# Layers 0 and 1 of an attention kernel: values of a context from one 80-row product, spread by a 0/1 tile, taken on ScalarE

## The chip, the cores and the metric

The kernel is one program on one core of a Trainium2 chip. The metric is device time in microseconds, the median of several executions. The core's engines each run their own instruction stream and meet through semaphores: TensorE (PE; its weight loads appear as PEld), VectorE (DVE), ScalarE (ACT), GpSimd (POOL) and SyncE (SP), which issues most DMAs.

## What is computed

The reference is four layers, each a cross attention and a feed-forward part with residuals, on x of 4 x 1024 x 256. Everything the change touches is in the attention of layers 0 and 1, on a context of 77 rows per batch:

```python
x = x + L0_xattn(layernorm(x), ctx, ctx, Wq, bq, Wk, bk, Wv, bv, Wo, bo)   # 16 heads of 16
x = x + L0_ffn(layernorm(x), ...)                                          # routed splines, gamma, beta
x = x + L1_xattn(layernorm(x), ctx, ctx, ...)                              # keys and values shared by the heads
# inside both attentions:
k = ctx @ Wk + bk ; v = ctx @ Wv + bv      # once per batch: 77 rows
attn = softmax(q @ k.T / 4) ; out = attn @ v
```

Layer 0 has 256 value columns (16 per head); layer 1 has 16, used by all heads. Layer 1's mask is causal. Layers 1 to 3 go on with two expert layers and a last attention; the change leaves them alone.

## The kernel before

`attention_layers` does layers 0 and 1. The 4096 rows of x are cut into 8 halves (NH = 8) of 512 tokens, two halves to a batch and so to a context. The program on every engine is the same double loop: `for h in range(-1, NH + 3)` and in it 16 slots (`PERIOD`), and each engine's code says what it issues in which slot. In round h, slots 0 to 7 hold the eight attention units of layer 0 on half h, slots 8 to 15 the eight units of layer 1 on half h-2 (rounds 0 and 1 have none there). A unit is 128 tokens by 8 heads: scores on TensorE (L176), maximum and shift on VectorE (L1007, L1008), exponential on ScalarE (L719), sums on VectorE (L1013, L1014), normalising on GpSimd (L631), five transposes on TensorE (L871), a copy to `PT` on ScalarE (L730), the value products on TensorE (L188) and a copy to `OT` on ScalarE (L726). The last four steps come two slots after the scores. Between the units lie the queries, norms and outputs: in slots 10 to 15 the output product of layer 0 (`project_out`, L840), the transposes of the next half's normalised rows (L826), the copy to `XT` (`take_xt`, L708), the query product (`project_q`, L833), its copy (`take_q`, L713), and the norm of the half's new rows (`ln_stats` L1018, `root` L698 on ScalarE, `ln_rstd` L1028 to L1033 on VectorE, `apply` L703 on ScalarE). Each round's norm "a" goes: statistics in slot 12, root in slot 13, `ln_rstd` in slot 13 behind `shift` and `sums`, `apply` in slot 14. GpSimd waits in slot 14 for `scale_by_gamma` (L1102), which VectorE issues in slot 13 behind `ln_rstd`.

Every instruction of an engine stands in line: a wait for one holds all behind it.

Keys and values of a context are made four times: for context 0 in round -1 (slots 0 to 5), and for contexts 1, 2, 3 in slots 10 to 15 of rounds 0, 2 and 4 (`context_of`). The value products of the units need the values of a context row repeated for 8 heads: 8 heads x 80 rows are 640 rows, in 5 blocks of 128 (`BLK`), so that each head's rows can be masked to that head's columns. Before the change this repetition is made at the input: `replicate` (L736, ScalarE) copies the transposed context 8 times to `crep`; `keys` on TensorE waits for it, makes the keys (L881, L883), the five 16-column value blocks of layer 1 (L887) and the last 256-column block of layer 0 (L889); `values` (L895) makes the other four blocks in two portions, two blocks in slot 12 and two in slot 14 (context 0: all in slot 4). Each block is two products, since the 256 inputs are two chunks of 128. ScalarE takes the keys (`take_keys`, L745, L746). VectorE takes the values with their bias to `vtmp` and `v1tmp` (`take_keys` and `take_values` there, L1120, L1126). GpSimd masks them to `Kbd` and `Vbd` (L649, L658, L668, L670) in the next round. All of these use the two banks called `wide` (SC). In the trace an f32 product is two MATMUL records, so L887 has 20 records a context, L889 4, L895 16.

The set-up block ahead of it loads the weights, and GpSimd makes masks there with `affine_select` (L476).

## Time and profile before

| | us |
|---|---|
| median of 3 executions | 2973.98 (2966.57 to 2975.74) |
| profiled execution, its time | 2977.86 |
| its span in the trace | 2976.1 |
| PE busy / DVE busy / ACT busy / POOL busy | 2417.7 / 1962.4 / 1508.6 / 809.2 |

Busy shares of the whole span say little here: the stages follow one another with barriers between, and the change lies in the first, from 28 to 776 us. Within it the starts of L1007 on VectorE, one per slot with a unit, are a clock by which slots can be compared between rounds: a round with a context (0, 2, 4) with one without.

### The profile page before, as it was taken

Reading aid. Unit: us, or ns where it says so; the run is one execution under the profiler, and the core shown is the slowest. Engines: PE = TensorE matmul, PEld = TensorE weight load, DVE = VectorE, ACT = ScalarE, POOL = GpSimd, SP = SyncE. Lnnn points to the kernel's source line nnn. Section 1 sums busy time; section 2 is a strip of 40 time slices with the busy share of each in tenths; the row PEclk is TensorE's granted clock in tenths of the full one; section 3 lists DMA queues with packets and bytes.
Section 4 is the critical chain, followed back from the end, with each engine's and each line's share of the span. In section 5 each row is a group of like instructions: output and inputs, shape, how many; then the busy total and the mean of one; then the engine's idle time right before and its main releaser. Section 6 shows DMA issues by size and latency. Waiting matters only on the chain. (4 is left out here: it accounts for less than half of the span.)

```text
span 2976.1 us, 43560 instructions
## 1 busy us (share of the span) xinstructions
PE 2417.7 (81%) x16502; PEld 1975.3 (66%) x16502; DVE 1962.4 (66%) x4449; ACT 1508.6 (51%) x2566; POOL 809.2 (27%) x707
## 2 busy tenths in 40 slices
PE   4778888877589999999849999999999276767665
PEld 3545554544477887888739999999999255555544
DVE  4688878875556666666526566666664468686867
ACT  2456667653445665565425444444543255545443
POOL 2233434432222433444440000000000572626030
PEclk9788888886699999999969999999999698988887
DMA  7500000000100111100014334333441511211000
GB/s 234 208 1 16 15 1 15 8 8 15 38 1 1 44 35 38 36 20 15 20 66 134 118 124 140 127 117 118 139 134 57 166 47 35 63 33 57 1 15 15
DMA packets 152616, 184.22 MB, mean 62 GB/s; under 512 B 21560, under 2 KB 118101, under 8 KB 152408
## 3 DMA queue, kind: packets, MB, share of 16 engines
q1 hardware_dynamic: 139400, 154.16, 15.8%
q0 software_dynamic: 12288, 27.15, 2.9%
q8 instruction: 132, 2.16, 0.3%
q14 instruction: 76, 0.62, 0.1%
q10 hardware_dynamic: 720, 0.12, 0.0%
HBM read 116.38 MB, written 71.43 MB: 63 GB/s over the span
## 5 line engine op out<-in xcount | busy, mean ns | idle before, releaser
L2355 POOL DMA_INDIRECT picked<-expert_out,so x128 | 126.8, 990 | 866.3 <-DMA so<-slots 765.1
L157 PE MATMUL SC<-Xhi,Whi 128*128 128x320 f32 x1024 | 319.9, 312 | 7.1 <-DVE Wlo L2148 5.3
L157 PE MATMUL SC<-Xlo,Whi 128*128 128x320 f32 x1024 | 316.9, 310 | 0.0
L157 PE MATMUL SC<-Xhi,Wlo 128*128 128x320 f32 x1024 | 316.9, 309 | 0.0
L631 POOL TENSOR_TENSOR PR<-PR,rs 128x616 f32<-128x616 f32 x128 | 157.8, 1233 | 410.0 <-DVE rs L1014 410.0
L1384 POOL TENSOR_TENSOR ff_Hlo<-ff_HF,ff_Hhi 128x512 fp32r<-128x512 f32 x112 | 148.0, 1322 | 419.4 <-ACT ff_Hhi L1517 419.3
L2125 ACT ACTIVATE Hhi<-HF 128x320 fp32r<-128x320 f32 x256 | 120.7, 471 | 154.7 <-DVE HF L2178 154.7
L157 PEld LDWEIGHTS SC<-Xhi,Whi 128*128 128x128 f32 x1024 | 193.0, 188 | 7.8 <-DVE Wlo L2148 5.7
L2167 DVE TENSOR_TENSOR Hlo<-HF,Hhi 128x320 fp32r<-128x320 f32 x256 | 125.5, 490 | 104.3 <-ACT Hhi L2125 104.3
L2148 DVE TENSOR_TENSOR Wlo<-Wraw,Whi 128x1024 fp32r<-128x1024 f32 x96 | 114.6, 1223 | 119.2 <-ACT Whi L2113 119.2
L157 PEld LDWEIGHTS SC<-Xlo,Whi 128*128 128x128 f32 x1024 | 193.1, 189 | 0.0
L157 PEld LDWEIGHTS SC<-Xhi,Wlo 128*128 128x128 f32 x1024 | 192.7, 188 | 0.0
L1784 DVE TENSOR_TENSOR ff_HF<-raw,SC 128x512 f32<-128x512 f32 x112 | 76.7, 685 | 168.3 <-ACT raw L1511 115.2
L157 PE MATMUL GP<-Whi,Hhi 128*128 128x256 f32 x640 | 181.8, 284 | 2.1 <-issue 2.1
L157 PE MATMUL GP<-Wlo,Hhi 128*128 128x256 f32 x640 | 181.8, 284 | 0.0
L157 PE MATMUL GP<-Whi,Hlo 128*128 128x256 f32 x640 | 181.8, 284 | 0.0
L176 PE MATMUL SC<-Kbd,QT 64*128 64x308 f32 x512 | 121.5, 556 | 66.3 <-DVE PR L1008 62.7
L2136 ACT ACTIVATE SG<-SC 128x320 f32<-128x320 f32 x256 | 111.5, 436 | 107.5 <-PE SC L157 107.5
L2178 DVE TENSOR_TENSOR HF<-SG,SC 128x320 f32<-128x320 f32 x256 | 124.2, 485 | 53.0 <-ACT SG L2136 52.8
L2113 ACT ACTIVATE Whi<-Wraw 128x1024 fp32r<-128x1024 f32 x96 | 97.3, 1048 | 115.6 <-PE GP L157 115.1
L871 PE MATMUL GP<-ident,PR 128*128 128x128 f32 x640 | 113.2, 317 | 44.1 <-ACT OT L726 27.6
L730 ACT ACTIVATE PT<-GP 128x640 f32<-128x640 f32 x128 | 89.5, 699 | 115.7 <-PE GP L871 115.3
(477 smaller groups left out, 6979.4 us busy)
## 6 DMA issues: line engine op xcount, KB each, us to landing
expert_in<-zeros SPq DMA_DIRECT2D x4, 5120.0 KB, 32.7
rowsin<-expert_in SPq DMA_DIRECT2D x32, 640.0 KB, 6.0
expert_out<-rowsout SPq DMA_DIRECT2D x32, 640.0 KB, 4.0
Wraw<-L_wg SPq DMA_DIRECT2D x32, 512.0 KB, 7.0
Wraw<-L_wu SPq DMA_DIRECT2D x32, 512.0 KB, 7.2
Wraw<-L_wd SPq DMA_DIRECT2D x32, 512.0 KB, 7.9
X<-x SPq DMA_DIRECT2D x8, 512.0 KB, 4.3
x_after_l_attention<-X SPq DMA_DIRECT2D x8, 512.0 KB, 2.8
```

Source lines behind the costliest of these rows:

```text
L157: last = nc.tensor.matmul(out, lhs[l], rhs[r], start=start and n == 0, stop=stop and n == 2)
L176: last = nc.tensor.matmul(o[j], q[r], K[r, 4 * j:4 * j + 4, 0:CTX], start=mask is None, stop=True)
L631: nc.gpsimd.tensor_tensor(pr, pr, bc_last(rs[n % NPA][:, :], CTX), mult).then_inc(pnorm, 1)
L871: last = nc.tensor.transpose(ptrans[:, k * P:(k + 1) * P], pr[:, k * P:(k + 1) * P], ident[:, :])
L1384: nc.gpsimd.tensor_tensor(lo[:, :], HF[q % 2][:, :], hi[:, :].bitcast(f32), ALU.subtract).then_inc(h_low, 1)
L2113: nc.scalar.activation(Wsp[j % 2][0][:, n, :], Wraw[j % 2][:, n, :], ACT.Copy).then_inc(w_high, 1)
L2125: nc.scalar.activation(Hsp[q // NU % 2][0][:, h, n * CC:(n + 1) * CC], HF[q % 2][:, :], ACT.Copy).then_inc(h_high, 1)
L2136: nc.scalar.activation(SG[u % 2][:, :], SC[u % 2][:, 0:CC], ACT.Silu).then_inc(s_ready, 1)
L2148: nc.vector.tensor_tensor(Wsp[j % 2][1][:, n, :], Wraw[j % 2][:, n, :], Wsp[j % 2][0][:, n, :].bitcast(f32), ALU.subtract)\
L2167: nc.vector.tensor_tensor(lo_, HF[q % 2][:, :], hi_.bitcast(f32), ALU.subtract).then_inc(h_made, 1)
L2178: nc.vector.tensor_tensor(HF[u % 2][:, :], SG[u % 2][:, :], SC[u % 2][:, 512:512 + CC], ALU.mult).then_inc(h_mult, 1)
L2355: nc.gpsimd.indirect_dma_start(picked[g][:, t, k, :], None, oute[:, :], bass.IndirectOffsetOnAxis(ap=so[g][:, t, k:k + 1], axis=0)).then_i ...
```

## The change

- `crep` and its copy are gone. A third product of `keys` multiplies the context itself (80 rows as output rows) with the value weights of both layers side by side (`wv`, 272 columns).
- VectorE adds the biases on the way to a tile `vctx` of 80 x 272 (`add_value_bias`, slot 12; context 0: slot 2), one instruction in place of three.
- A 0/1 tile `spread` of 80 x 5 x 128, made in the set-up block, repeats the rows: `last_values` (slot 12; context 0: slot 3) makes the last block of layer 0 and the five of layer 1, `values` (slot 14; context 0: slot 4) the other four blocks, all in one go and only when ScalarE has taken what `last_values` made.
- ScalarE takes the values: `take_last_values` in slot 13 and `take_values` in slot 15; its `take_keys` goes from slot 11 to 12, behind `take_xt` (context 0: slots 3, 5 and 2).
- `ln_rstd` of norm "a" on VectorE goes from slot 13, behind `shift` and `sums`, to the head of slot 14, ahead of `shift`; `scale_by_gamma` stays in slot 13.

```diff
                     def keys(b):
-                        pe.wait_ge(crep_ready, b + 1)
+                        if b:
+                            pe.wait_ge(ctx_in, 16 * b)
...
-                        for j in range(BLK):
-                            for k in range(KC):
-                                nc.tensor.matmul(wide[:, V1AT + j * DH:V1AT + (j + 1) * DH], rep(j, k), wv1[:, k, :], start=k == 0, stop=k == KC - 1)
                         for k in range(KC):
-                            last = nc.tensor.matmul(wide[:, TOK:TOK + D], rep(BLK - 1, k), wv0[:, k, :], start=k == 0, stop=k == KC - 1)
+                            last = nc.tensor.matmul(wide[0:CTXP, TOK:TOK + D + DH], ctxT[:, k, :], wv[:, k, :], start=k == 0, stop=k == KC - 1)
                         last.then_inc(k_psum, 1)
-                    def values(j0, j1):
-                        for j in range(j0, j1):
-                            for k in range(KC):
-                                last = nc.tensor.matmul(wide[:, j * D:(j + 1) * D], rep(j, k), wv0[:, k, :], start=k == 0, stop=k == KC - 1)
-                        return last
+                    def last_values(b):
+                        pe.wait_ge(vctx_ready, b + 1)
+                        nc.tensor.matmul(wide[:, TOK:TOK + D], spread[:, BLK - 1, :], vctx[:, 0:D], start=True, stop=True)
+                        for j in range(BLK):
+                            last = nc.tensor.matmul(wide[:, V1AT + j * DH:V1AT + (j + 1) * DH], spread[:, j, :], vctx[:, D:], start=True, stop=True)
+                        last.then_inc(v4_psum, 1)
+
+                    def values(b):
+                        pe.wait_ge(kcol_ready, b + 1)
+                        pe.wait_ge(v4_taken, b + 1)
+                        for j in range(BLK - 1):
+                            last = nc.tensor.matmul(wide[:, j * D:(j + 1) * D], spread[:, j, :], vctx[:, 0:D], start=True, stop=True)
+                        last.then_inc(v_psum, 1)
...
+                    def take_last_values(b):
+                        act.wait_ge(v4_psum, b + 1)
...
+                        nc.scalar.activation(vtmp[:, BLK - 1, :], wide[:, TOK:TOK + D], ACT.Copy)
+                        nc.scalar.activation(v1tmp[b % 2][:, :, :], wide[:, V1AT:V1AT + BLK * DH].rearrange("p (j d) -> p j d", d=DH), ACT.Copy)\
+                            .then_inc(v4_taken, 1)
+                    def take_values(b):
+                        act.wait_ge(v_psum, b + 1)
+                        nc.scalar.activation(vtmp[:, 0:BLK - 1, :], wide[:, :].rearrange("p (j d) -> p j d", d=D), ACT.Copy).then_inc(v_taken, 1)
...
+                for h in range(HH):
+                    keep_where(spread[:, :, :], [[P, BLK], [1, P]], -CTXP * h, -1, ALU.not_equal, 1.0)
...
+                            if s == 14 and 0 <= h < NH:
+                                ln_rstd(h, LN["a"], var_a, sd_a, rstd_a)
                             if now is not None:
                                 shift(now)
```

On TensorE in round 4 (context 3), slots 11 to 12, what stood in a row before:

```order
L881 MATMUL SC1<-ctxT,wk0 128x80 x4
L883 MATMUL SC1<-ctxT,wk1r 128x80 x2
L887 MATMUL SC1<-wv1,crep 128x16 x10
L889 MATMUL SC1<-wv0,crep 128x256 x2
L871 MATMUL GP0<-ident,PR2 128x128 x5
```

and what stands there now:

```order
L892 MATMUL SC1<-ctxT,wk0 128x80 x4
L894 MATMUL SC1<-ctxT,wk1r 128x80 x2
L897 MATMUL SC1<-wv,ctxT 80x272 x2
L884 MATMUL GP0<-ident,PR2 128x128 x5
```

Twelve products became two; six new ones (L902, L904) stand one slot later, behind the transposes of `XP`, where four of L895 stood.

On ScalarE in the same round, slots 11 to 14, before (PR0 is the unit of slot 12, PR1 of slot 13; `root` is L698):

```order
L745 ACTIVATE kcol0<-SC1,bk0c 128x80 x2
L746 ACTIVATE kcol1_1<-SC1,bk1c 128x80
L703 ACTIVATE XN_1<-XN_1,nm_g,rstd_g 128x256 x4
L730 ACTIVATE PT<-GP0 128x640
L719 ACTIVATE PR0<-PR0 128x8x77
L726 ACTIVATE OT_1<-GP0 128x128
L708 ACTIVATE XT<-GP1 128x1024
L730 ACTIVATE PT<-GP0 128x640
L698 ACT_TABLE_LOAD
L698 ACTIVATE sd_a<-mv_a,eps 128x4
```

and now, to the same root:

```order
L706 ACTIVATE XN_1<-XN_1,nm_g,rstd_g 128x256 x4
L733 ACTIVATE PT<-GP0 128x640
L722 ACTIVATE PR0<-PR0 128x8x77
L729 ACTIVATE OT_1<-GP0 128x128
L711 ACTIVATE XT<-GP1 128x1024
L742 ACTIVATE kcol0<-SC1,bk0c 128x80 x2
L743 ACTIVATE kcol1_1<-SC1,bk1c 128x80
L733 ACTIVATE PT<-GP0 128x640
L701 ACT_TABLE_LOAD
L701 ACTIVATE sd_a<-mv_a,eps 128x4
```

The taking of the keys went from ahead of `XN_1`, PT and the exponential to behind `XT`; `crep` (one slot earlier, L736) is gone.

On VectorE in the same round, slots 13 and 14, now (before, L1028 to L1033 stood ahead of `XN_1` times gamma, and L1007 behind it):

```order
L1116 TENSOR_TENSOR XN_1<-XN_1,gammar 128x1024
L1042 RECIPROCAL rstd_a<-sd_a 128x4
L1043 TENSOR_TENSOR nw_a<-rstd_a 128x4
L1044 SCALAR_TENSOR_TENSOR nw_a<-mv_a,nw_a 128x4
L1045 TENSOR_SCALAR nw_a<-nw_a 128x4
L1046 TENSOR_TENSOR rstd_a<-rstd_a,nw_a 128x4
L1047 SCALAR_TENSOR_TENSOR nm_a<-mv_a,rstd_a 128x4
L1021 TENSOR_REDUCE mx<-SC0 128x8
```

Only the product with gamma passed the norm; the norm's place to the next `shift` is the same.

## Rows read from the trace of the kernel before

**Rows 1.** Busy by stretch: start:end, length, busy of each engine, clock, DMA
```profile
28.00:776.00 748.00, 587.49 (x4384) 377.66 (x4384) 567.54 (x1329) 434.19 (x735) 264.86 (x212) 0.84 0.13 47
```

**Rows 2.** Waits of 28 to 776: waiter, released by, total us, times, longest
```profile
ACT kcol L745 <- PE SC L889: 23.0, 4, 7.5
...
DVE rstd_a L1028 <- ACT sd_a L698: 20.5, 8, 6.4
```

**Rows 3.** Groups by line and shape: busy, mean ns, idle before them
```profile
L708 ACT ACTIVATE XT<-GP 128x1024 f32<-128x1024 f32 x24 | 24.6, 1025 | 24.9 <-PE GP L826 24.8
...
L736 ACT ACTIVATE crep<-ctxT 128x1280 f32<-128x1280 f32 x4 | 5.0, 1258 | 0.0
```

**Rows 4.** Timeline of context 0: start, us, engine, what [idle before]
```profile
26.68 1.41 DVE L1018 BATCH_NORM_STATS2 stats_p<-X 128x6 f32<-128x256 f32 x4 [0.90 <-PEq L79]
...
30.04 2.00 PE L881 MATMUL SC<-ctxT,wk 128*128 128x80 f32 x8 [5.42 <-ACT crep L736]
30.14 2.07 ACT L703 ACTIVATE XP<-X,nm_p,rstd_p 128x256 f32<-128x256 f32 x4 [0.15 <-DVE nm_p L1033]
...
32.68 4.37 PE L887 MATMUL SC<-wv,crep 128*128 128x16 f32 x20
...
36.88 2.05 PE L889 MATMUL SC<-wv,crep 128*128 128x256 f32 x4
...
41.31 3.70 PE L833 MATMUL GP<-XT,wq 128*128 128x512 f32 x8 [1.11 <-ACT XT L708]
...
48.40 0.79 PE L176 MATMUL SC<-Kbd,QT 64*128 64x308 f32 x4
```

**Rows 5.** Timeline of round 4, slots 12 to 14 (context 3)
```profile
388.65 0.80 DVE L1007 TENSOR_REDUCE mx<-SC 128x8 f32<-128x616 f32 x1 [0.32 <-PE SC L176]
...
390.51 2.34 PE L887 MATMUL SC<-wv,crep 128*128 128x16 f32 x20
...
393.85 0.55 ACT L745 ACTIVATE kcol<-SC,bk0c 128x80 f32<-128x80 f32 x2 [4.33 <-PE SC L889]
...
396.12 0.77 DVE L1007 TENSOR_REDUCE mx<-SC 128x8 f32<-128x616 f32 x1
...
407.50 0.79 DVE L1007 TENSOR_REDUCE mx<-SC 128x8 f32<-128x616 f32 x1
...
410.47 1.99 PE L895 MATMUL SC<-wv,crep 128*128 128x256 f32 x8
...
410.79 2.06 ACT L703 ACTIVATE XN<-X,nm_a,rstd_a 128x256 f32<-128x256 f32 x4
```

**Rows 6.** Timeline of round 5, slots 12 to 14 (no context)
```profile
474.84 0.79 DVE L1007 TENSOR_REDUCE mx<-SC 128x8 f32<-128x616 f32 x1
...
479.00 0.77 DVE L1007 TENSOR_REDUCE mx<-SC 128x8 f32<-128x616 f32 x1
...
483.32 0.18 DVE L1028 RECIPROCAL rstd_a<-sd_a 128x4 f32<-128x4 f32 x1 [1.78 <-ACT sd_a L698]
...
485.54 0.79 DVE L1007 TENSOR_REDUCE mx<-SC 128x8 f32<-128x616 f32 x1
...
485.98 1.27 ACT L713 ACTIVATE QT<-GP,bq0c 128x512 f32<-128x512 f32 x2 [0.56 <-PE GP L833]
```

**Rows 7.** Timeline of round 0, slots 12 to 14 (context 1)
```profile
88.48 1.01 PE L881 MATMUL SC<-ctxT,wk 128*128 128x80 f32 x8
...
99.20 1.89 PE L895 MATMUL SC<-wv,crep 128*128 128x256 f32 x8
...
104.91 1.28 ACT L719 ACT_TABLE_LOAD   x1
```

**Rows 8.** Timeline elsewhere: a slow query product, and the set-up block's masks
```profile
5.25 0.26 POOL L476 TENSOR_SCALAR_AFFINE_SELECT causal<-causal 128x77 bf16<-128x77 bf16 x1
...
6.21 0.10 POOL L493 MEMSET edge<- 128x1 f32 x1
...
665.57 6.42 PE L833 MATMUL GP<-XT,wq 128*128 128x512 f32 x8 [1.11 <-ACT XT L708]
```

More of the change, by code:

```diff
@@ L395, in attention_layers @@
         causal = sb("causal", [P, CTX], bf16)
-        crep = sb("crep", [P, KC, HH, CTXP])
+        spread = sb("spread", [CTXP, BLK, P])
+        vctx = sb("vctx", [CTXP, D + DH])
         vtmp = sb("vtmp", [P, BLK, D])
@@ L478, in _ @@
                 for t, v in ((ident[:, :], 0.0), (identb[:, :], 0.0), (headof[:, :], 1.0), (blockhead[:, :, :], 1.0),
-                             (onesf[:, :], 1.0), (onesb[:, :], 1.0), (before[:, :], 1.0), (causal[:, :], 0.0)):
+                             (onesf[:, :], 1.0), (onesb[:, :], 1.0), (before[:, :], 1.0), (causal[:, :], 0.0),
+                             (spread[:, :, :], 0.0)):
                     link(nc.gpsimd.memset(t, v))
@@ L802, in _ @@
                                 take_one_hot(c1)
-                            if s == (0 if c == 0 else 10) and c is not None:
-                                replicate(c)
                             if p < NH and s == query_slot(p, "apply"):
                                 apply(p, rstd_p, XP, X[p % NXA], LN["p"], xn_p)
-                            if s == (1 if c == 0 else 11) and c is not None:
-                                take_keys(c)
                             if s == 11 and 0 <= c1 < NH:
@@ L818, in _ @@
                                 take_xt(h, xt_a_psum, xt_a)
+                            if s == (2 if c == 0 else 12) and c is not None:
+                                take_keys(c)
+                            if s == (3 if c == 0 else 13) and c is not None:
+                                take_last_values(c)
+                            if s == (5 if c == 0 else 15) and c is not None:
+                                take_values(c)
                 @block.tensor
@@ L872, in unit_transposes @@
                         last.then_inc(pt_psum, 1)
[L874 to L875 removed]
                     def keys(b):
[L878 removed]
+                        if b:
+                            pe.wait_ge(ctx_in, 16 * b)
                         for c in range(KC):
@@ L984, in _ @@
                                 project_q(wq0, p, xt_p, q0_psum)
-                            if s == (4 if c == 0 else 12) and c is not None:
-                                pe.wait_ge(kcol_ready, c + 1)
-                                values(0, BLK // 2)
+                            if s == (3 if c == 0 else 12) and c is not None:
+                                last_values(c)
                             if s == (4 if c == 0 else 14) and c is not None:
-                                pe.wait_ge(v4_taken, 2 * (c + 1))
-                                values(BLK // 2, BLK - 1).then_inc(v_psum, 1)
+                                values(c)
                             if s == 15 and 0 <= h < NH:
@@ L1165, in _ @@
                                 ln_stats(XN[c1 % G], LN["g"], var_g)
-                            if s == (5 if c == 0 else 15) and c is not None:
-                                take_values(c, 0, BLK - 1, wide[:, :], v_psum, v_taken)
                             if s == 10 and 0 <= c1 < NH:
@@ L1174, in _ @@
                                 ln_stats(X[h % NXA], LN["a"], var_a)
-                            if s == 13 and 0 <= h < NH:
-                                ln_rstd(h, LN["a"], var_a, sd_a, rstd_a)
                             if s == 13 and 0 <= c1 < NH:
```

55 lines of the change are left out of this document (22 added, 33 removed).

## The prediction, written before the changed kernel was run

> **What bounds the kernel now.** I read the busy times by stretch first. In the stage of layers 0 and 1, 748 us of the span, PE is busy 587 us, DVE 568, ACT 434 [rows 1]: no engine is full, so the stage is a ring of waits, and what counts is where each wait ends last. The starts of L1007 show the ring's pace. In round 5, without a context, slot 12 takes 4.2 us (474.84 to 479.00) and slot 13 takes 6.5 (to 485.54) [rows 6]; in round 4, with one, the same slots take 7.5 and 11.4 [rows 5]. Round 2 reads like round 4. So a context costs about 8.2 us in each of these two rounds, whichever engine does its work. The waits name the places: ACT waits 23.0 us in four times for the last product of `keys`, DVE 20.5 us in eight times for the root of norm "a" [rows 2], and PE 5.42 us once for `crep` [rows 4]. The stage's end is a barrier, so what is gained up to there is gained to the end.
>
> **Removed work.** Per context PE loses 20 records of L887, 4 of L889 and 16 of L895, and gains 4 (272 columns), 2 (256), 10 (16) and 8 (256). At the rates of round 4 a 16-column record takes 0.117 us (2.34 for 20) and a 256-column record 0.24 (1.99 for 8, with its end) [rows 5]. In `keys` 24 records (2.3 + 0.9 = 3.2 us) become 4 of about 0.25, 1.0 us: 2.2 us less ahead of everything in slot 12. `last_values` is 2 x 0.24 + 10 x 0.117 = 1.6 us, `values` 8 x 0.24 = 1.9. A contraction over 80 rows in place of 128 is not in the trace; its record is bounded by the 16-column one (0.117) and the 256-column one at the slow rate (0.51, from 2.05 for 4 [rows 4]); I take 0.24, since the moving columns are the same. ACT loses `crep` (1.26 us) and gains takes of 256, 80 and 1024 columns. 1024 columns cost 1.02 us [rows 3]; the small two lie between 0 and 1.02 together, and I take 0.7 by columns and a fixed part. DVE exchanges three instructions for one.
>
> **Context 0, term 1.** PE starts 30.04, after 5.42 us of idling for `crep` [rows 4]. Without `crep` it starts when the block does, about 26.7, as DVE's L1018 shows [rows 4]. Keys take 2.0 + 1.1 us, the new product 2.0 at the slow rate seen here: done at 31.8. The transposes of XP wait for ACT's L703, which doesn't move (30.14 to 32.21 [rows 4]); they run 32.3 to 33.8, XT is taken by 34.9, the query product runs 3.7 us to 38.7, `last_values` to 40.3, its takes to 41.1, `values` to 43.1. The first scores start at 43.1 in place of 48.40 [rows 4]: 5.3 us. ACT's `take_values` (1.0 us) and its table load lie beside the scores and `shift`. What may eat into it is PE's clock: the first 8 us of this stretch ran at half speed, L887 taking 4.37 us for 20 records [rows 4] where round 4 takes 2.34 [rows 5]. If the query product, `last_values` and `values` ran so, it would cost 6.42 - 3.70 = 2.7 [rows 4, 8], 1.5 and 1.5: 5.7 us. Between 0 and 5.7 I take 1.0, since L833 ran at 3.70 after a wait of 1.11 [rows 4]. **Term 1: -4.3 us** (0 to -5.3).
>
> **Context 1, term 2.** Round 0 has no units in slots 8 to 15, so this is a bare chain. `keys` ends 2.1 us sooner, at 91.0 (it starts 88.48 [rows 7], which doesn't move: `project_out` ends there). Transposes of XP to 91.9, `last_values` to 93.4, XT to 92.9, keys taken by 93.9, query product 93.4 to 97.1, its take to 98.5. Only then comes ACT's `take_last_values`, to 99.2, and `values` on PE waits for it, for its banks: it starts at 99.2, where the second portion of L895 starts now [rows 7]. The 2.1 us are lost in that wait. Behind it ACT has `apply` and XT about 1.0 us sooner, and then `take_values` with 1.02 us ahead of the table load at 104.91 [rows 7]. **Term 2: 0 us** (-1 to +1.5).
>
> **Contexts 2 and 3, term 3.** Followed in round 4. `keys` is done at 391.7 in place of 393.8. ACT no longer waits 4.33 us for it ahead of XN, PT and the exponential [rows 5]: XN runs 389.6 to 391.6, PT to 393.0, exponential to 393.7, OT to 394.1. PE: values of the unit to 393.8, XP to 394.8, `last_values` to 396.3. ACT: XT to 395.9, keys to 396.8. Slot 13: PE transposes to 397.1, ACT PT to 397.8, root with its table load to 399.4, load and exponential to 401.4; PE's query product 398.5 to 402.2; ACT takes it by 403.5, then the small value takes, 0.7, to 404.2, where `take_last_values` now stands ahead of PT. Slot 14: PT to 404.9, exponential to 405.6, PE's unit products to 405.6, `values` to 407.3 (its wait is long over), OT, and `apply` of norm "a" starts at 406.0 in place of 410.79 [rows 5]: 4.8 us. In slot 15 ACT gets `take_values`, 1.02 us [rows 3], ahead of slot 0's PT: 3.85 us remain. The chain from there to the next round runs on ACT, through XT, PT and root "c", so DVE's larger gain (it loses L1120) isn't added. Bounds: 0, if the new takes hold ACT as long as the wait did; 8.2, if a context came to cost nothing. **Term 3: 2 x -3.85 = -7.7 us** (0 to -16.4).
>
> **The norm a slot later, term 4.** In round 5 DVE waits 1.78 us at L1028 [rows 6] with the product with gamma (1.2 us) behind it. Now the product fills the wait, and `shift` of slot 14 starts 1.1 us sooner. But ACT in slot 14 starts with L713 at 485.98, after 0.56 us of idling for PE's L833 [rows 6], and then takes PT and the exponential; L833 depends on XT, not on this norm. What DVE gains ends in its wait for the exponential or for root "c". In round 4 the wait of 6.4 us [rows 2] is part of term 3. **Term 4: 0 us** (0 to 8 x -1.1 = -8.8, the lower end if it all passed on).
>
> **At nothing.** GpSimd makes `spread` with one memset and 8 selects of 640 columns; 77 columns cost 0.26 us [rows 8], so at most 8 x 2.2 = 17.6 us if it goes by columns alone. GpSimd has finished its masks at 6.3 [rows 8], and the set-up block, which waits for the weights, holds PE's work until 24.6 (30.04 less 5.42): 18.3 us of cover. Without it, it would be 2 (8 x 0.26) to 17.6 us. The split load of `wv` moves the same bytes. SP's `context` wait comes sooner, with nothing behind it that was late.
>
> **Sum.** -4.3 + 0 - 7.7 + 0 = **-12.0 us** against the profiled execution's own 2977.86, so 2965.9; that execution lies 3.9 us above the median of the runs shown, so the forecast against the median is 2962.0.
>
> **Rivals.** (A) *The norm's 1.1 us passes on in all eight rounds*: -8.8 more, 2953. For it: DVE's 20.5 us of waiting [rows 2]. Against: ACT's slot 14 starts on PE. 13%. (B) *ACT becomes the bound in rounds 2 and 4*: the new takes stand ahead of PT and XT there, and gain is left of about 1 us each: -4.3 - 2 = -6.3, 2968. For it: `apply`, XT, PT, exponential already stand in a row; against: the 4.33 us wait goes for certain. 22%. (C) *Not what it says at the start*: the block is held by something else than `crep`, term 1 is 0: -7.7, 2966. 5%. (D) *Slower*: the engine that loses 20 us of work falls to half clock at the contexts. Then the query product, `last_values` and `values` cost 5.7 us more at each of the four, all on the chain: 22.8 against the undiscounted 13.0, +9.8, 2984. It decides from three of four contexts on. For it: L833 at 6.42 us late in the stage, behind waits [rows 8]; against: rounds without a context have less PE work in these slots and L833 there runs 3.7. 5%.
>
> The Trainium skill, page "TensorE: Matmul & The Clock Gate", section "Loop structure matters more than you think", says that a stretch in which TensorE idles brings its clock back down, which speaks against a change that takes work from it. By that rule, the trace agrees at 665.57 us, where L833 took 6.42 us behind a wait, and not at 41.31, where it took 3.70 behind one as long. By the page case (D) would be the outcome and the sum +9.8; by the rows of context 0 it isn't.
>
> **How the numbers follow.** The forecast has 55%, with its own range of 2957 to 2967 (term 1 and term 3 within a third). The range for 8 in 10 goes from 2951 (case A with its undiscounted start, and the spread of the medians) to 2971 (case B with term 1 at its small end), leaving out (D). 0.3% is 8.9 us, about what a measurement of this kernel can tell from no change: faster by more holds A and nine tenths of the forecast and a little of C, 66%; within 0.3% holds B, C and the forecast's rest, 28%; slower 6%.
>
> **What the profile after would show.** Term 1: first scores (L176) near 43 to 45, PE's first product before 28. Term 2: exponential's table load in round 0 behind the first scores by about 4 us, as now. Term 3: slots 12 and 13 of rounds 2 and 4 at together 13 to 16 us in place of 19; the waits for L889 gone. Term 4: rstd_a waits under 5 us in all, while rounds 3 and 5 keep their length of 78 to 79 us. If plain rounds get shorter, (A); if rounds 2 and 4 keep 19 us, (B); if L833 reads above 5 us at the contexts, (D).

## The result, and the profile after

| | before | after |
|---|---|---|
| median | 2972.61 (2965.56 to 2975.74) | 2947.76 (2940.64 to 2950.61) |
| ratio | | 0.992 [0.9903, 0.9937] |
| profiled execution, its time / span | 2977.86 / 2976.1 | 2950.61 / 2948.8 |

All times are us; each side has five executions. The change is faster by 0.8%, 24.9 us between the medians; the forecast was 2962.0 and the range ended at 2951, so the result lies outside it, on the fast side. Two more comparisons with copies of both kernels, each on one chip (below), give 18.7 and 19.5 us, 0.62% and 0.69%.

The stage of layers 0 and 1 is the part of the program that the change edits. Its busy times after, by stretch (start:end, length, busy of PE, PEld, DVE, ACT, POOL with counts, granted clock, DMA share, GB/s):

```profile
28.00:764.00 736.00, 573.49 (x4317) 362.81 (x4316) 562.98 (x1322) 434.95 (x743) 270.20 (x212) 0.84 0.14 49
```

Beside [rows 1] PE has 14 us less work and DVE 5 less, ACT has as much as before, at the same mean clock. The waits of the same stretch (waiter, releaser: total, times, longest):

```profile
ACT PT L733 <- PE GP L884: 114.9, 69, 5.0
...
DVE rstd_c L1042 <- ACT sd_c L701: 20.4, 8, 4.7
...
DVE rstd_a L1042 <- ACT sd_a L701: 6.5, 6, 1.8
```

ACT's wait for the last product of `keys`, 23.0 us in [rows 2], doesn't appear any more; DVE's wait for the root of norm "a" went from 20.5 us to 6.5. Context 0 after (start, us, engine, line, idle before with its releaser):

```profile
27.06 1.97 PE L892 MATMUL SC<-ctxT,wk 128*128 128x80 f32 x8 [2.06 <-PEq L79]
...
29.68 2.02 PE L897 MATMUL SC<-wv,ctxT 128*80 128x272 f32 x4
...
32.65 1.97 PE L839 MATMUL GP<-ident,XP 128*128 128x128 f32 x8 [0.95 <-ACT XP L706]
...
35.73 6.03 PE L846 MATMUL GP<-XT,wq 128*128 128x512 f32 x8 [1.11 <-ACT XT L711]
...
41.59 0.60 PE L902 MATMUL SC<-vctx,spread 80*128 80x256 f32 x2
...
42.03 1.18 PE L904 MATMUL SC<-vctx,spread 80*128 80x16 f32 x10
...
43.91 1.97 PE L911 MATMUL SC<-vctx,spread 80*128 80x256 f32 x8 [0.69 <-ACT v1tmp L752]
...
45.80 0.79 PE L176 MATMUL SC<-Kbd,QT 64*128 64x308 f32 x4
```

Beside [rows 4]: PE starts 3.0 us earlier, as it should without `crep`, but the first scores come only 2.6 us earlier, 45.80 for 48.40: the query product, 3.70 us before, takes 6.03. Round 4, slots 12 to 14, after:

```profile
379.62 0.80 DVE L1021 TENSOR_REDUCE mx<-SC 128x8 f32<-128x616 f32 x1 [0.32 <-PE SC L176]
...
381.48 1.08 PE L897 MATMUL SC<-wv,ctxT 128*80 128x272 f32 x4
...
384.68 0.77 DVE L1021 TENSOR_REDUCE mx<-SC 128x8 f32<-128x616 f32 x1
...
386.52 0.54 ACT L742 ACTIVATE kcol<-SC,bk0c 128x80 f32<-128x80 f32 x2
...
388.98 3.70 PE L846 MATMUL GP<-XT,wq 128*128 128x512 f32 x8
...
391.15 0.80 DVE L1021 TENSOR_REDUCE mx<-SC 128x8 f32<-128x616 f32 x1
...
393.87 0.38 ACT L751 ACTIVATE vtmp<-SC 128x256 f32<-128x256 f32 x1
394.13 0.25 ACT L752 ACTIVATE v1tmp<-SC 128x80 f32<-128x80 f32 x1
...
395.91 2.06 ACT L706 ACTIVATE XN<-X,nm_a,rstd_a 128x256 f32<-128x256 f32 x4
```

Slots 12 and 13 take 5.1 and 6.5 us, 11.5 together, where they took 7.5 and 11.4 in [rows 5]; `take_keys` (L742) waits for nothing; `apply` of norm "a" starts 16.3 us after slot 12 and not 22.1.

**Where the time went**, from the starts of the slots' first instructions (L1007 before, L1021 after; a round is taken at its slot 1, rounds 8 and 9 at slot 8; the last mark before the span's end is ScalarE's first instruction of the next stage). Each number is how much earlier than before that point comes:

| point | before | after | earlier by |
|---|---|---|---|
| first `shift` | 49.6 | 46.6 | 3.0 |
| round 1 | | | 3.4 |
| round 2 / round 3 | | | 2.3 / 7.2 |
| round 4 / round 5 | | | 8.7 / 14.1 |
| rounds 6, 7, 8, 9 | | | 13.9, 16.4, 12.9, 15.1 |
| next stage begins | 780.3 | 764.8 | 15.5 |
| end of the span | 2976.1 | 2948.8 | 27.3 |

Rounds 2 and 4, which hold contexts 2 and 3, gain 4.9 and 5.4 us; the start 3.0; context 1 0.4; the rest moves to and fro by up to 3.5 and adds up to 1.8. That is 15.5 us in the edited stage. The other 11.8 of the profiled pair lie behind it, in stages that no edit touches (start:end as above, the next stage in both kernels and then the last):

```profile
780.30:1535.70 755.40, 669.91 (x3748) 567.22 (x3748) 470.14 (x1543) 410.53 (x621) 290.76 (x240) 0.94 0.08 25
...
2314.80:2976.10 661.30, 430.73 (x3042) 309.56 (x3042) 461.11 (x795) 301.33 (x533) 238.34 (x221) 0.86 0.16 48
```

```profile
764.80:1517.60 752.80, 668.10 (x3748) 566.44 (x3748) 469.65 (x1543) 410.47 (x621) 290.46 (x240) 0.94 0.08 26
...
2296.10:2948.80 652.70, 430.73 (x3042) 310.89 (x3042) 461.23 (x795) 300.47 (x533) 237.79 (x221) 0.85 0.16 48
```

The instruction counts are the same, PE's busy time in the last stage is the same to 0.01 us, and yet it is 8.6 us longer in the execution of before. Of the seventeen profiled executions of this study, only that one shows a last stage over 654.

### The profile page after: what moved, and what is told of

It is laid out like the page before. It is cut to its first block and busy times, and to the rows that moved or that the text cites. A ratio compares the mean times of both kernels' runs of the same rounds, so it can differ in the third digit from the quotient of the medians.

```text
span 2948.8 us, 43447 instructions
## 1 busy us (share of the span) xinstructions
PE 2401.7 (81%) x16438; PEld 1960.9 (66%) x16438; DVE 1957.3 (66%) x4441; ACT 1508.3 (51%) x2574; POOL 820.3 (28%) x716
## 3 DMA queue, kind: packets, MB, share of 16 engines
q1 hardware_dynamic: 139304, 154.11, 15.9%
## 5 line engine op out<-in xcount | busy, mean ns | idle before, releaser
L2360 POOL DMA_INDIRECT picked<-expert_out,so x128 | 126.4, 987 | 864.7 <-DMA so<-slots 764.5
```

The source lines that it names most:

```text
L2360: nc.gpsimd.indirect_dma_start(picked[g][:, t, k, :], None, oute[:, :], bass.IndirectOffsetOnAxis(ap=so[g][:, t, k:k + 1], axis=0)).then_i ...
```

## The experiments

Fifteen kernels ran, in four groups; those of a group ran on the same chip and share the executions of before. Each ratio is against before in that group. "Stage" is the end of layers 0 and 1 in the profiled execution: 780.3 before, 764.8 after.

### Group 1: taking the change apart

**e1_norm_only**, the kernel before with norm "a" a slot later:

```diff
+                            if s == 14 and 0 <= h < NH:
+                                ln_rstd(h, LN["a"], var_a, sd_a, rstd_a)
                             if now is not None:
                                 shift(now)
...
-                            if s == 13 and 0 <= h < NH:
-                                ln_rstd(h, LN["a"], var_a, sd_a, rstd_a)
```

> The kernel before, with only the norm of each round (ln_rstd of norm a) moved to the head of slot 14. Theory 1 (what VectorE gains ends in ScalarE's chain): rounds 3 and 5 keep 78 to 79 us, the whole 0 to 2 us under the kernel before. Theory 2 (the 1.1 us passes on in each of eight rounds, rival A): 9 us under it, the rounds near 77.5. If the later stages, which no edit touches, are shorter by 9 to 12 us here too, they are so whatever is edited.

Measured: 2963.44, ratio 0.9981 [0.997, 0.9992]; stage ends at 773.9. From slot 12 to slot 1 of the next round, the plain round 3 takes 22.9 us in place of 23.4, the context rounds 31.1 in place of 31.2. It is a small gain in plain rounds and hardly any where a context is; the ratio lies between the two recorded theories (0 to 2 us, and 9). The stage ends 6.4 us sooner, more than these rounds add up to, although its first scores come 1.7 us later (the query product takes 5.34 us here, see group 4). But e10 below, the kernel before with nothing changed behind the set-up block, also ends its stage 4.4 us sooner, so the length of this one stage can't be read as the norm's worth.

**e2_no_norm**, the changed kernel with the norm back in slot 13 (the same four lines, reversed):

> The changed kernel with the norm back in slot 13. Theory 1: within 2 us of the changed kernel, so 23 to 25 us under the kernel before; in rounds 2 and 4 slot 13 stays long, as the root comes late, but the chain runs on ScalarE. Theory 2: 9 us above the changed kernel.

Measured: 2949.1, 0.9938 [0.9917, 0.9958]; stage ends at 764.1, against 764.8 with the norm moved. The median is 19.0 us under that of before, where 23 to 25 were expected. Everything else of the change holds its gain without it: the moved norm is worth nothing that can be seen in the median or the stage's end. It isn't a clean nothing: this execution's start was 2.3 us shorter by TensorE's clock (first `shift` at 44.3 for 46.6, group 4), and from there on the stage takes 719.8 us against 718.2.

**e3_dve_takes**, the changed kernel with the same two takes as copies on VectorE, in the same slots:

```diff
-                        nc.scalar.activation(vtmp[:, 0:BLK - 1, :], wide[:, :].rearrange("p (j d) -> p j d", d=D), ACT.Copy).then_inc(v_taken, 1)
+                        nc.vector.tensor_copy(vtmp[:, 0:BLK - 1, :], wide[:, :].rearrange("p (j d) -> p j d", d=D)).then_inc(v_taken, 1)
```

> The changed kernel with the values taken by VectorE copies, in the same slots (13 and 15; 3 and 5 at the start). Theory 1 (ScalarE's chain is the bound in rounds 2 and 4, and the takes there cost 1.7 us each): 2 to 4 us faster than the changed kernel, if VectorE's slots stay beside it. Rival (VectorE is the bound): 2 to 4 us slower.

Measured: 2948.23, 0.9929 [0.9914, 0.9945]; the stage ends at 759.4, 5.4 us before that of the changed kernel. Slot 12 to slot 1 of the context rounds is 24.6 us, against 26.4. Of the 5.4 us, 0.9 stand at the start, where TensorE's clock rose sooner; from the first `shift` on the stage takes 713.7 us against 718.2, and in the two later pairs with and without these takes 711.0 against 721.4 (e11, e9) and 708.0 against 711.6 (e15, e14). In the median it can't be told from its neighbours. So in the traces one of the moves in the change costs: the takes on ScalarE stand ahead of `PT`, and in slot 15 ahead of the next one. VectorE has room there (round 4 of this kernel):

```profile
394.44 1.23 DVE L1130 COPY vtmp<-SC 128x1024 f32<-128x1024 f32 x1 [0.67 <-PE SC L893]
```

It waits 0.67 us for the product and copies in 1.23. ScalarE's take of the same tile lasts 1.02, but on the chain.

**e4_with_crep**, the changed kernel in which ScalarE still makes `crep`, that nobody reads, and the first products still wait for it:

```diff
-                        if b:
-                            pe.wait_ge(ctx_in, 16 * b)
+                        pe.wait_ge(crep_ready, b + 1)
```

> The changed kernel with the copy of the context for 8 heads (nobody reads it) made again on ScalarE, and the first products waiting for it as before. Term 1 (the start): the first scores come 3.0 to 3.4 us later than in the changed kernel, and the rest is unchanged, since at rounds 0, 2 and 4 the copy lies beside the output product: 3 to 4 us slower than the changed kernel. If the gain at the start came from less work of keys alone, 0 to 1 us.

Measured: 2950.9, 0.9936 [0.9918, 0.9953]; stage ends at 762.4. Its start:

```profile
29.71 2.00 PE L900 MATMUL SC<-ctxT,wk 128*128 128x80 f32 x8 [5.41 <-ACT crep L740]
...
34.17 1.91 PE L848 MATMUL GP<-ident,XP 128*128 128x128 f32 x8
37.20 3.70 PE L855 MATMUL GP<-XT,wq 128*128 128x512 f32 x8 [1.11 <-ACT XT L713]
...
46.30 1.40 PE L176 MATMUL SC<-Kbd,QT 64*128 64x308 f32 x4
```

PE starts 2.65 us later than in the changed kernel, and its first scores come only 0.5 us later, 46.30 for 45.80, since the query product takes 3.70 us here. At the first `shift` it is 1.1 us behind, since its first scores run at half clock (1.40 us for 0.79). Its stage even ends 2.4 us sooner than that of the changed kernel, where 3 to 4 us later were expected: a miss. So most of what removing the wait for `crep` gave at PE's start was lost to a slower clock, and no run here shows a gain of it at the stage's end. Groups 3 and 4 are on that clock.

### Group 2: the order alone, and how far executions repeat

**e5_before_again** and **e6_after_again** are copies of the two kernels.

> The kernel before, unedited, as a second trace of it. The question is the 12 us by which the first trace of it was longer in the stages that nothing edits. Theory 3 (they vary from execution to execution, with TensorE's clock): its feed-forward stage of layers 1 and 2 reads 753 to 764 us and the last stage 652 to 661, in any pairing, with slots in layers 0 and 1 as in the first trace. Theory 4 (the change shortens them): last stage 661 again, where all changed kernels so far read 653.

> The changed kernel, unedited, as a second trace, on the chip of the second trace of before. Theory 3: stage of layers 0 and 1 13 to 17 us shorter than in the kernel before, medians 15 to 20 us apart. Theory 4: medians 22 to 26 us apart again.

Measured: 2965.03, 0.9991 [0.9976, 1.0005], for before, and 2949.18, 0.9938 [0.9917, 0.9958], for after. The stage ends at 780.0 and 764.1, so the 15.5 of the first pair is 15.9 here: this part repeats within 1 us. The next stage does not. In the copy of before it takes 761.1 us, in that of after 752.7:

```profile
780.00:1541.10 761.10, 676.19 (x3748) 573.07 (x3748) 469.55 (x1543) 410.44 (x621) 290.49 (x239) 0.93 0.08 25
```

```profile
764.10:1516.80 752.70, 668.04 (x3748) 565.99 (x3748) 469.72 (x1543) 410.53 (x621) 290.53 (x239) 0.94 0.08 26
```

PE is busy 8.1 us more with the same number of records, at a lower mean clock: the stage takes 752 to 755 us or about 762 (761.1 to 763.7), which differ in how long TensorE ran at 1.2 GHz.

**e7_order_only**, the kernel before with the new order alone: `take_keys` behind `take_xt` and all four blocks of `values` in slot 14.

```diff
-                            if s == (1 if c == 0 else 11) and c is not None:
-                                take_keys(c)
...
+                            if s == (2 if c == 0 else 12) and c is not None:
+                                take_keys(c)
...
-                            if s == (4 if c == 0 else 12) and c is not None:
-                                pe.wait_ge(kcol_ready, c + 1)
-                                values(0, BLK // 2)
```

> The kernel before with its own products and crep, but ScalarE's take_keys in slot 12 behind take_xt (slot 2 at the start) and all of values in slot 14: the order of the change without its smaller products. If the gain of 5.0 us in rounds 2 and 4 is mostly the order (ScalarE no longer waits 4.33 us for keys), slots 12 to 15 fall from 31.2 us (to slot 1 of the next round) to 27 to 28; if it is the smaller products, they stay at 30 to 31.

Measured: 2966.99, 0.9993 [0.998, 1.0006]; stage ends at 778.4. From slot 12 to slot 1, a context round takes 28.6 us in place of 31.4 (expected 27 to 28 if it is mostly the order), but context 1 takes 1.0 us more (31.6 for 30.6 from slot 7 of round 0 to round 1). The order alone leaves 1.6 to 1.9 us of gain in the stage.

**e8_keys_slot11**, the changed kernel with `take_keys` back where it was, in slot 11:

> The changed kernel with take_keys back in slot 11 (slot 1 at the start): the smaller products without the order. ScalarE then waits about 2.2 us for the product of 272 columns in place of 4.33. If the order was the gain, rounds 2 and 4 read 28 to 29 us from slot 12 to the next slot 1; if the products were, 26.4 as in the changed kernel.

Measured: 2949.53, 0.994 [0.9919, 0.9962]; stage ends at 763.1. Slot 12 to slot 1 takes 28.4 us. With before at 31.4, the change without the new place of `take_keys` gives 3.0, the order alone (e7) 2.8, the whole 5.0, so they overlap by 0.8. It isn't a pure split: e8 keeps the takes on ScalarE, the moved norm and all of `values` in slot 14, and the last of these is in e7 too. All the same this kernel's stage isn't longer than that of the changed one. Its start is 1.1 us shorter, and the 2 us that each of its context rounds loses come back elsewhere in the stage. It ran more at full clock: from 44 us to the stage's end, half clock is granted for 219 us of it, in the two executions of after for 237 and 243.

### Group 3: TensorE's clock at the start

Theory: the missing 2 us of the start are TensorE's clock. Dead products of 512 columns, whose result nobody reads, keep it at work in the set-up block, where it waits for weights anyway.

```diff
                 pe.wait_ge(made, 1)
+                for i in range(8):
+                    nc.tensor.matmul(SC[0][:, 0:512], ident[:, :], bc_at(ident[:, :], 1, 4), start=True, stop=True)
                 pe.wait_ge(quant, 1)
```

> The changed kernel with eight dead products of 512 columns on TensorE in the set-up block (as soon as GpSimd's masks are there, 10.8 us) and one behind the block's last transposes; they are ahead of context 0 and add no wait to it. Theory (the start's missing 2 us is TensorE's clock: it comes from idling at half speed, and the query product of context 0 takes 6.03 us for 8 records in place of 3.70): with work ahead of it the granted clock of 27 to 45 us is full, the query product takes 3.70, the new product of 272 columns 1.1 in place of 2.02, and the first scores start at 42 to 43 in place of 45.80; the stage from there on is as long as before, 718 to 719 us, and the kernel's time 2 to 3 us less. Rival (the clock of the start does not hang on what TensorE did ahead of it): the query product stays at 5.3 to 6.4 us and the first scores at 44 to 46.

> The kernel before with dead products of 512 columns on TensorE in the set-up block, thirteen from the moment of the masks (4 us) and one behind the last transposes. Theory: the keys and values of context 0, 8.9 us at half clock from 30.0, take 4.9 to 5.2, and the first scores start at 44 to 45 in place of 48.40, so 4 us are gained; the start's gain of the change between two kernels at full clock is then about 2 us, not 5.3. Rival (the clock does not hang on it): 20 records of 16 columns stay at 4.4 us, the first scores at 48.

> The changed kernel with the values taken by VectorE and not ScalarE, and with the dead products in the set-up block: both things that took from the gain put right. Theory: the gains add, the last expert-free point of the stage (first piece of the next layer's tile made on ScalarE) comes at 756 to 758 us in place of 764.1 to 764.8, and the median is 5 to 8 us under that of the changed kernel. Rival (what is gained in the stage of layers 0 and 1 is given back in the later stages, whose length varies between executions by 12 us): the stage is shorter by as much, the median within 2 us of the changed kernel.

> The changed kernel once more, for comparison with the three beside it and for how far its stages repeat: query product of context 0 at 5.3 to 6.1 us, first scores at 44 to 46, layers 0 and 1 done at 764 to 765, the next stage at one of its two lengths, 752 to 755 or 761 to 764, the expert stage at 778.4 to 779, and a median 16 to 20 us under the kernel before on this chip.

Measured: e9 2951.51, 0.9948 [0.9928, 0.9967]; e10 2964.64, 0.9991 [0.9977, 1.0005]; e11 2942.71, 0.9919 [0.9899, 0.9939]; e12 2947.56, 0.9931 [0.9911, 0.9951]. In e9 the keys and the new product ran at full rate, 1.09 and 1.08 us for 1.97 and 2.02; the query product did not:

```profile
27.85 1.08 PE L900 MATMUL SC<-wv,ctxT 128*80 128x272 f32 x4
...
32.06 1.65 PE L842 MATMUL GP<-ident,XP 128*128 128x128 f32 x8 [3.13 <-ACT XP L709]
34.83 5.89 PE L849 MATMUL GP<-XT,wq 128*128 128x512 f32 x8 [1.11 <-ACT XT L714]
...
44.76 0.79 PE L176 MATMUL SC<-Kbd,QT 64*128 64x308 f32 x4
```

TensorE now needed 2.2 us less for them, and then waited 3.13 us for the normalised rows. The granted clock of PE fell in that place (start:end, length, busy, granted clock, DMA share, GB/s):

```profile
28.00:32.00 4.00, 0.93 (x5) 1.00 1.01 350
32.00:34.00 2.00, 1.65 (x8) 0.61 1.08 318
34.00:38.00 4.00, 3.17 (x4) 0.50 1.09 291
```

So both expectations were half right: behind work the clock was full, but it was lost again in a gap, and the first scores, expected at 42 to 43, came at 44.76; nor is the median lower than that of e12. From there on the stage took 721.4 us where the changed kernel takes 718.2: two further spells at half clock, between 97 and 108 us, stand where the changed kernel ran at full. In e10 TensorE waited 4.06 us behind the dead products and 4.03 for `crep`; its granted clock, 1.00 from 18 to 22 us, is 0.50 from 24 to 38, the 20 records of 16 columns take 4.37 us as before, the first scores came at 48.73, and the expected 44 to 45 was a miss.

e11 came out at the lowest median of the study, 4.9 us under e12 on the same chip, with the stage ending at 757.2 as expected; the two intervals overlap. e12 repeats the changed kernel: stage at 764.5, query product 6.06 us, first scores 45.47.

### Group 4: the gap filled

The same dead products right behind the keys of context 0: one in e13 (nothing in the set-up block), three in e14 and e15 (with those of group 3; e15 with the takes on VectorE too).

```diff
                         last.then_inc(k_psum, 1)
+                        if b == 0:
+                            for i in range(3):
+                                nc.tensor.matmul(pscores[:, 0:512], ident[:, :], bc_at(ident[:, :], 1, 4), start=True, stop=True)
```

> The changed kernel with one dead product of 512 columns on TensorE behind the keys of context 0, so that it does not wait there (0.95 us) for the normalised rows; nothing in the set-up block. Theory (TensorE comes to full clock only after it has worked almost without gaps; in the kernel before it had, from 30.0 to 39 us): the transposes come 1 us later, but the query product, from about 36.4, runs at full clock for most of its length, 3.7 to 4.7 us in place of 6.03, and the first scores start at 44 to 45. Rival (the half-clock query product has another cause): it stays at 5.9 to 6.1 and the first scores come at 46.5, 1 us later than without the dead product.

> The changed kernel with the dead products of the set-up block and three more behind the keys of context 0, which fill the 3.1 us in which TensorE waited there. Theory (the wait brought the clock down at 33 us): the clock stays full through the query product, it takes 3.7 us, the first scores start at 42.3 to 43 in place of 44.76, and of the layers' stage the part from there is 718 to 721 us. Rival (what brings the clock down is the work itself, a budget spent in the set-up block): the query product takes 5.9 us or more, the first scores come at 44.5 to 45.5, as without the three.

> As the one before, and the values taken by VectorE and not ScalarE. Theory (the gains add): the expert-free point at the end of layers 0 and 1 at 754 to 756 us (757.2 with warm products alone, 764.5 for the changed kernel), median 2939 to 2942. Rival (half-clock spells later in the stage take it back): 757 or more, and the median 2943 to 2947.

Measured: e13 2948.16, 0.9932 [0.9912, 0.9952]; e14 2944.65, 0.9926 [0.9906, 0.9947]; e15 2942.91, 0.9926 [0.9904, 0.9947]. The start of e13:

```profile
29.21 1.71 PE L897 MATMUL SC<-wv,ctxT 128*80 128x272 f32 x4
30.75 1.02 PE L901 MATMUL SC<-ident 128*128 128x512 f32 x2
32.19 1.09 PE L839 MATMUL GP<-ident,XP 128*128 128x128 f32 x8 [0.41 <-ACT XP L706]
34.40 3.70 PE L846 MATMUL GP<-XT,wq 128*128 128x512 f32 x8 [1.11 <-ACT XT L711]
...
40.24 3.30 PE L914 MATMUL SC<-vctx,spread 80*128 80x256 f32 x8 [0.69 <-ACT v1tmp L752]
43.48 1.40 PE L176 MATMUL SC<-Kbd,QT 64*128 64x308 f32 x4
```

With one product that is of no use, 1.02 us long, the query product takes 3.70 us in place of 6.03; the first scores come at 43.48, 2.3 us earlier than in the changed kernel. The recorded numbers came true, but the reason isn't shown, and looks like luck. The new product's four records take 1.71 us in place of 2.02: the last of them, from 30.5, runs at full rate, so the rise came before the dead product began at 30.75. And e2, whose program on TensorE is that of the changed kernel, rose in the same place without any dead product:

```profile
28.99 1.85 PE L897 MATMUL SC<-wv,ctxT 128*80 128x272 f32 x4
31.97 1.10 PE L839 MATMUL GP<-ident,XP 128*128 128x128 f32 x8 [1.13 <-ACT XP L706]
34.18 5.27 PE L846 MATMUL GP<-XT,wq 128*128 128x512 f32 x8 [1.11 <-ACT XT L711]
...
43.49 0.79 PE L176 MATMUL SC<-Kbd,QT 64*128 64x308 f32 x4
```

Its first scores come at 43.49, as early as those of e13. The reverse stands in e1, which has the start of the kernel before, with no gap at all between 29.69 and 40.3 us:

```profile
38.38 1.91 PE L826 MATMUL GP<-ident,XP 128*128 128x128 f32 x8
41.41 5.34 PE L833 MATMUL GP<-XT,wq 128*128 128x512 f32 x8 [1.11 <-ACT XT L708]
```

All starts without dead products ahead, by the moment from which TensorE's records run at full rate (from the spacing of single records in the traces, us):

| start of | executions | first product | full rate from | query product, its time | first scores |
|---|---|---|---|---|---|
| before | before, e5, e7 | 29.8 to 30.0 | 39.6, 40.6, 41.1 | 41.3 to 41.5, 3.70 | 48.4 to 48.6 |
| before | e1 | 29.7 | 44.8 | 41.4, 5.34 | 50.1 |
| changed | after, e6, e12 | 26.3 to 27.1 | 39.7 to 40.5 | 35.0 to 35.7, 6.03 to 6.06 | 45.1 to 45.8 |
| changed | e3, e8 | 26.3, 26.4 | 38.5, 38.8 | 35.0, 35.1; 5.41, 5.50 | 44.5, 44.7 |
| changed | e2 | 26.4 | 30.5, half again 34.0 to 37.4 | 34.2, 5.27 | 43.5 |
| with `crep` | e4 | 29.7 | 36.7 | 37.2, 3.70 | 46.3 |
| gap filled | e13 | 26.6 | 30.5 | 34.4, 3.70 | 43.5 |

So what the traces show is this: in eight of the ten executions with the start of either kernel the full rate comes at 38.5 to 41.1 us, and the change moves the query product from 41.3, behind that moment, to 35.0 to 35.7, ahead of it. The moment itself varies between like starts, from 39.6 to 44.8 and from 30.5 to 40.5. Whether the gap of 0.95 us puts it off is not shown: one execution with the gap rose at 30.5, one without any rose only at 44.8. The start of e14:

```profile
28.78 2.74 PE L904 MATMUL SC<-ident 128*128 128x512 f32 x6
32.08 1.09 PE L842 MATMUL GP<-ident,XP 128*128 128x128 f32 x8 [0.56 <-ACT XP L709]
34.28 3.70 PE L849 MATMUL GP<-XT,wq 128*128 128x512 f32 x8 [1.11 <-ACT XT L714]
...
42.03 0.79 PE L176 MATMUL SC<-Kbd,QT 64*128 64x308 f32 x4
```

```profile
32.00:34.00 2.00, 1.09 (x8) 1.00 1.11 329
34.00:38.00 4.00, 3.72 (x9) 1.00 1.16 299
```

With the gap filled the granted clock stays at 1.00 where it was 0.50 in e9, and the start is 2.7 us shorter than in e9. e11 and e15 are a second such pair (6.15 and 3.70), and e2 and e13 go the same way: both rose at 30.5, e2 with gaps of 1.13 and 1.11 us fell again at 34.0, e13 with gaps of 0.41 and 1.11 not before 40.7. That settles one half: from full clock the idle gap brings it down, not the work spent ahead of it. The other half, when the clock rises from a cold start, as in the changed kernel, stays open.

What is gained at the start isn't always kept. In e13 the clock falls at 41 us (L914 takes 3.30 us for 1.97), and the stage from the first `shift` on takes 720.2 us, against 718.2: its end, 765.1, is no earlier than that of the changed kernel. In e14 it takes 711.6, where 718 to 721 were expected, and the stage ends at 754.5; in e15 it ends at 751.7, 12.8 us before e12. The half-clock time from 44 us to the stage's end is 253 us in e13, 224 in e14 and e15, 263 in e9 (added up over stretches of 4 us), 237 to 243 in the three executions of the changed kernel, and 246 and 234 in the two of before. It goes along with these lengths only in part: e4, the same program from there on, has 244 us and takes 714.7. So kernels that are alike behind the start differ by up to 10 us in this stage, from 711.6 to 721.4, and single stages of e3, e11, e14 and e15 are to be read with that spread. Why one start leads to fewer such spells hundreds of us later is not shown here.

Nor do the medians follow the stage in full: e15 is 4.7 us below e12, of 12.8 in the profiled executions, and they are of two groups. e11, e14 and e15 may be some us faster than the changed kernel; their intervals overlap with its own, so it isn't shown.

## Why the prediction was wrong

The forecast was -12.0 us, the range to 2951. The median after lies 14.2 us under the forecast of 2962.0: 3.7 of them in the edited stage (-15.7, the mean of the two pairs), 9.2 behind it, and 1.4 because before has a median of 2972.6 over five executions and not 2974.0. The direction and the places of the gains were right. Two steps failed for the time. The larger: the sum stopped at the stage's barrier ("what is gained up to there is gained to the end") and put the stages behind it at nothing, without any spread; they took 2195.8 us before and 2184.0 after in the profiled pair, 11.8 of its 27.3 us. The smaller: term 3, -3.85 us a context, measured -5.15. A third step, term 1's discount for the clock, failed the other way and had the start too good.

**Term 1, -4.3 forecast, -3.0 measured** at the first `shift`, -4.0 in the second pair (49.87 to 45.90); at the first scores 2.6 and 3.6. PE's start (27.06 for about 26.7) and the absence of the `crep` wait are as told. The step that failed is the discount of 1.0 us for the slow clock, taken because L833 had run at 3.70 us "after a wait of 1.11". That row stands at 41.31, behind the rise of the clock at 39.6. The forecast moved the product to 34.9, into a stretch in which the prediction's own rows run at half rate (L887 and L889, until 38.9 [rows 4]), and kept the rate of the old place. In the changed kernel the clock rises at 39.7 to 40.5 in three executions, and the product costs 2.3 us more. That is a part of case (D), at context 0 alone and in the term's bounds. e4 and e13 alone would suggest that the gap of 0.95 us ahead of the transposes keeps the clock down; e1 and e2 don't bear that out, and what sets the moment of the rise stays open. The rule quoted from the Trainium skill, page "TensorE: Matmul & The Clock Gate", section "Loop structure matters more than you think", that idling brings the clock back down, the traces bear out where it had been up: in e9 a gap of 3.13 us took it from 1.00 to 0.50, and e14 without that gap kept it. In the changed kernel's own start it had not yet been up; and at contexts 2 and 3 it stayed up, L846 takes 3.70 us there.

**Term 2, 0 forecast, -0.4 measured.** Right: `values` waits there for the takes. e7 shows the other side of it, +1.0 us when the order changes without the cheaper products.

**Term 3, -7.7 forecast, -10.3 measured** (4.9 and 5.4). Mechanism right, size short by 1.3 us a context; slots 12 and 13 take 11.5 us together where 13 to 16 were named. `apply` of norm "a" was forecast 4.8 us sooner and came 5.85 sooner: the query product started 9.4 us behind slot 12's start in place of my 9.85; the two small takes, priced 0.7 us "by columns and a fixed part", hold up `PT` for 0.38 (393.87 to 394.25), since each starts before the one ahead of it has ended; and the steps behind them were 0.3 us shorter in all. Of that, `take_values` took back 0.9 us, priced at 1.02. What I took for 80-row products was right: L904 takes 1.18 us for 10 records and L911 1.97 for 8, as the products of 128 rows did (L887 2.34 for 20, L895 1.99 for 8 [rows 5]). e7 and e8 bear on the split: 2.8 us by the order alone, 3.0 by the change without the new place of `take_keys`, 5.0 together.

**Term 4, 0 forecast.** Right as far as the runs can tell: in e2, without it, the stage ends 0.7 us earlier, with a start that was 2.3 us shorter by the clock, so up to 1.6 us of this one execution may be the norm's. In plain rounds slot 12 to slot 1 is 0.4 us shorter (22.9 for 23.4), where (A) wanted 1.1; and the rstd_a wait is 6.5 us in place of "under 5". On the kernel before it gives 0.19% (e1), which can't be seen on top of the rest of the change.

**At nothing.** GpSimd's masks, with `spread`, are done at 14.1 us in place of 6.3: 7.8 us more, within the 2 to 17.6, and still ahead of PE's start, as told.

**The cases.** (A) came nearest in time, 2953, with the wrong reason. (B), ScalarE as the bound, is out as a bound, but e3 shows that the takes there cost 1.8 us in each of these rounds: a part of it was true and hidden behind a larger gain. (C) is out: PE starts at 27.06.

**What lies outside.** The medians differ by 24.9 us in the first comparison, 18.7 and 19.5 in the two repeats, the edited stage by 15.5 and 15.9 in the two pairs that have a trace of both. So 3 to 9 us come from elsewhere. Of the profiled executions, those of before and of the kernels made from it (before, e1, e5, e7, e10) take 2182.1 to 2196.2 us behind the stage, mean 2190.6; those of after and its kin (twelve) 2181.4 to 2193.8, mean 2184.5, with the 762-us length of the next stage only in e4, against e1 and e5 of the five. The work there is the same to the record. That the changed kernels fall less often into the long length would account for the 3 to 9 us, but twelve and five executions don't prove it, and what chooses the length wasn't tried. This stays open. The range was too narrow on that side: it gave the unchanged stages no spread, while two executions of one kernel differ by up to 16 us.

## What to carry to other kernels

Where an engine stands on a ring of waits, price a removed wait by the step that follows it on the same engine, and price small takes by when the next instruction may start, not by their own length. Where a change moves a long TensorE product towards the start of a program, price it at the rate that the rows around its new place show, not at that of its old one: here it came 6 us sooner, ahead of the clock's rise, and took 6.03 us for 3.70. Where the clock is up, look for gaps: one of 3.13 us took it down, and useless products in the gap kept it. An expected number that comes true (e13) isn't the mechanism: look at whether the effect starts behind its cause, and in the traces of the other kernels. And before a small difference of two kernels is put down to the edit, compare the stages that the edit doesn't touch; here they held almost half of the first pair's difference.

## What the runs showed of the hardware

- At the start the column of the granted clock reads 1.00 while the records run at half rate: in the changed kernel 4 records of 272 columns take 2.02 us at 29.68, and 1.08 in round 4, though its row from 26 to 42 us reads

```profile
26.00:42.00 16.00, 12.87 (x34) 1.00 0.90 257
```

  In e9, which had worked from 14 us on, the same column shows the fall to 0.50. So in these traces, until the first rise, the durations of like records tell the clock (1.2 GHz), and the column doesn't.
- The first rise to full rate varies between executions with the same start: 39.6 to 44.8 us with the start of the kernel before (four executions), out of an unbroken run of work from about 30; with the start of the changed kernel 38.5 to 40.5 in five executions and 30.5 in one, behind a first product at 26.3 to 27.1.
- From full rate, gaps of 3.13 us (e9, e11) and 4.06 us (e10) each went with a fall to half. With the gap of 3.13 filled down to 0.56 (e14, e15) the rate stayed up until 46 us.
- A stage of identical work (the one behind layers 0 and 1) took 751.8 to 755.4 us in fourteen profiled executions and 761.1 to 763.7 in three, in which TensorE was granted 1.2 GHz for longer; the last stage once took 661.3 in place of 650 to 654.
- Products with 80 rows and 256 or 16 columns take as long as with 128 rows (at full rate 1.97 us for 8 records against 1.99, and 1.18 for 10 against 2.34 for 20).
- ScalarE's take of 128 x 1024 from PSUM lasts 1.02 us and VectorE's copy 1.23; the one on the engine with room was the cheaper by 1.8 us a context round (e3).
